# Three pairs of PSUM banks in the shared expert, and the last expert weights issued by SyncE

## The chip, the cores and the metric

The kernel runs on one core of a Trainium2 chip. A core has TensorE (matrix products into PSUM, eight banks), VectorE, ScalarE, GpSimd and SyncE, each with a queue of its own, and 16 DMA engines that all queues share. The metric is the device time of one execution in microseconds. The kernel before took 493.1 us (median of 3 runs, 491.43 to 493.35).

## The reference

Two cross-attention layers and two feed-forward layers over x of 2 x 1024 rows of 256 numbers. The change lies in the first feed-forward layer, a mixture of experts with a shared expert:

```python
gu = jnp.einsum('nh,eih->nei', x_flat, experts_gate_up)
g, u = (gu[..., :I], gu[..., I:])                      # I = 352, 8 experts, 2 chosen per row
h = jax.nn.silu(g) * u
expert_out = jnp.einsum('nei,ehi->neh', h, experts_down)
out = jnp.einsum('neh,ne->nh', expert_out, w)
shared = jax.nn.silu(x_flat @ shared_gate_w.T) * (x_flat @ shared_up_w.T) @ shared_down_w.T
out = out + sigmoid(x_flat @ shared_expert_gate_w.T) * shared   # 704 hidden columns
```

Everything is float32. The kernel writes each factor as the sum of a high and a low part in a faster format and adds three products.

## The kernel before

All queues are written out by hand. The 2048 rows are taken in four groups of 512. For the shared expert, a group has six steps (n counts them, 0 to 23): five of 128 hidden columns, with a gate and an up product of six matmuls each, and a half step (n = 5, 11, 17, 23) whose last 64 gate and 64 up columns share one product. `up(n)` issues them on TensorE (L1232, the half step L1226). Gate products go to bank n % 2 and up products to bank 2 + n % 2. In the first half (n below 12) ScalarE computes the silu (L1131) and copies the up product (L1137), and GpSimd multiplies. In the second half VectorE multiplies (L1475) the up product in its bank by the silu in SBUF. `down(g)` is the down product of a group (L1285), `add` the sum into x (L1426). down(0), steps 12 and 13, down(1), steps 14 to 23, down(2), down(3) follow each other on TensorE. Beside steps 12 to 23 GpSimd scatters the rows by expert into DRAM (`expert_rows_in`, 32 indirect DMAs, L1063).

The experts come next, in 39 blocks of 128 rows. For block b TensorE transposes the fetched rows (L960), ScalarE copies them as the high part (L966) and VectorE makes the low part (L971). `half` makes the gate, and later the up product: four matmuls with the high part (L1336, L1337) and two with the low part (L1340). ScalarE applies the silu (L1162), VectorE multiplies (L1496), TensorE transposes the result (L1348) and makes the down product (L1358 to L1362). TensorE's order in a turn is: gate of b, transposes of the hidden values of b - 1, transposes of the rows of b + 1, up product of b, down product of b - 1.

SyncE fetches the rows of a block (L953) and its weights and destinations (L954) into four buffers in turn: the fetch of block b waits for the transposes of block b - 4. The expert weights lie over buffers of the shared stage and so are loaded late. ScalarE's queue issues them (`load_w` L930, `load_d` L937): experts 0 to 3 after the last gate product, 4 after VectorE's last product, 5 after the scatters, and 6 and 7 after all down products (`d_ready` 16), behind the copy of block 0's rows and ahead of the first silu. GpSimd's queue loads the high parts of the down weights (L937). The low parts are made by a subtraction: of gate and up by L942, of down by L948, for expert 0 on VectorE, and else mostly on GpSimd.

Of the kernel before, what the change touches and what calls it, by code (L numbers as in the profile page):

```python
# [7 lines left out]
ALU = mybir.AluOpType  # L8
# [4 lines left out]
P = 128  # L13
# [15 lines left out]
KS = 6  # L29
# [25 lines left out]
def wait(engine, sem, value):  # L55

    if isinstance(value, int) and value <= 0:
        return
    if isinstance(sem, Event):
        engine.wait_ge(sem.sem, sem.before + value)  # L60
    else:
        engine.wait_ge(sem, value)
# [603 lines left out]
def xattn_ffn_kernel(nc, x_in, ctxT_in, wq0, wk0, wv0, wo0, gate_in, egu_in, edown_in, sgate_in, sup_in, sdown_in,  # L666
                     wq1, bq1, wk1, bk1, wv1, bv1, wo1, bo1, wr_in, a_in, bw_in, out):
    ctx = ExitStack()
    with ctx:
# [203 lines left out]
        NH = 2 * KS  # L873
        HIGH = slice(SR[5], P)

        def up_at(n):

            return (psum[n % 2], HIGH) if n % KS == KS - 1 else (psum[2 + n % 2], slice(0, P))

        def factor_rows(n):  # L880

# [2 lines left out]
        def ups(n):  # L884

            return n - n // KS
        act_s, up_s = mem["pw"][:, 0:2, :], mem["pw"][:, 2:4, :]
        hT = big[:, 0:2 * KS * SG].rearrange("p (b j n) -> p b j n", b=2, j=KS)

        xg = mem["xn"][:, :, :, :].rearrange("p b t n -> p (b t) n")  # L890
# [83 lines left out]
        def sync_on():  # L974
# [11 lines left out]
            sp.wait_ge(scattered, 16 * 2 * NT)  # L986
            for b in range(NX):
                fetch(sp, b)
            for b in range(NX, NB):
                fetch(sp, b)  # L990

# [131 lines left out]
        def scalar_on():  # L1123
            act = nc.scalar
            def silu(n):
                wait(act, g_ready, n + 1)
                if n < NH + 2:
                    wait(act, h_done, n - 1)
                else:
                    wait(act, h2_done, n - 1 - NH)  # L1130
                nc.scalar.activation(act_s[factor_rows(n), n % 2, :], psum[n % 2][0:SR[n % KS], :], ACT.Silu).then_inc(silu_done, 1)  # L1131

            def copy_up(n):

# [47 lines left out]
            load_w(act, 5, 6, w_in[4])  # L1182
            load_d(act, 5, 6, 1, w_in[4])
            copy_rows(0)
            act.wait_ge(d_ready, 16)
            load_w(act, 6, E, w_in[5])
            load_d(act, 6, E, 1, w_in[5])
            for b in range(NB):
                silu_rows(b)
                if b > 0:  # L1190
# [22 lines left out]
        def up(n):  # L1213

            g, j = n // KS, n % KS
            if g < 2:
                wait(nc.tensor, xL_ready, 2 * g + 2)
            wait(nc.tensor, silu_done, n - 1)
            if n < NH + 2:
                wait(nc.tensor, u_copied, n - 1)  # L1220
            else:
                wait(nc.tensor, h2_done, n - 1 - NH)
            terms = [(m, v, k) for k in range(KD) for m, v in ((sgu_hi, xn2T_hi), (sgu_hi, xn2T_lo), (sgu_lo, xn2T_hi))]
            if j == KS - 1:
                for a, (m, v, k) in enumerate(terms):
                    last = nc.tensor.matmul(psum[n % 2][:, :], m[:, k, 5 * P:6 * P], v[g][:, k, :],  # L1226
                                            start=(a == 0), stop=(a == len(terms) - 1))
                last.then_inc(g_ready, 1)
                return
            for w, bank, done in ((0, n % 2, g_ready), (1, 2 + n % 2, u_ready)):  # L1230
                for a, (m, v, k) in enumerate(terms):
                    last = nc.tensor.matmul(psum[bank][:, :], m[:, k, w * 6 * P + j * P:w * 6 * P + (j + 1) * P],  # L1232
                                            v[g][:, k, :], start=(a == 0), stop=(a == len(terms) - 1))
                last.then_inc(done, 1)

# [169 lines left out]
        def vector_on():  # L1405
# [64 lines left out]
            def hidden(n):  # L1470
                bank, rows = up_at(n)
                wait(dve, silu_done, n + 1)
                wait(dve, u_ready, ups(n + 1))
                wait(dve, d_ready, 4 * (n // KS - 1))
                v.tensor_tensor(hT[0:SR[n % KS], (n // KS + 1) % 2, n % KS, :], bank[rows, :],  # L1475
                                act_s[rows, n % 2, :], ALU.mult).then_inc(h2_done, 1)

            add(0)
            for n in range(2 * KS, 2 * KS + 2):
# [418 lines left out]
```

## Time and profile before

| | |
|---|---|
| median of 3 runs | 493.1 us (491.43 to 493.35) |
| profiled execution | 497.36 us, span 495.5 us |
| mean granted TensorE clock | 0.992 |
| TensorE busy (matmul) | 468.4 us, 95% of the span |
| VectorE, ScalarE, GpSimd busy | 58%, 40%, 48% |
| share of the DMA engines, 198 to 235 us | near full |

The profile comes from one execution. A timeline row gives the start, the length, the engine and line, the operation, and in brackets how long the engine stood idle before it and who released it. "remote" and "another core or an unknown queue" are releases that the profile can't assign. ACTq, POOLq and SPq are DMA issues of the queues of ScalarE, GpSimd and SyncE.

### The profile page before, as it was taken

The numbers are of one execution on the slowest core, as the hardware profiler recorded it, in microseconds if no ns is written. First come the engines' busy times: TensorE is split into PE (matmuls) and PEld (weight loads), VectorE is DVE, ScalarE is ACT, GpSimd is POOL, SyncE is SP. The second block draws the span as 40 slices with busy tenths as digits, with TensorE's granted clock in tenths as the row PEclk, the third lists the DMA queues.
The fourth block names the chain that finished last, engine by engine and source line by source line (L and its number), as shares of the span: only waits on it lengthen the run. The fifth ranks groups of instructions, "written<-read, shape, count | busy, mean of one in ns | idle before, by whom it ended". The sixth has DMA issues, their size and how long they took to land.

```text
span 495.5 us, 9491 instructions
## 1 busy us (share of the span) xinstructions
PE 468.4 (95%) x3132; PEld 385.0 (78%) x3132; DVE 286.6 (58%) x657; ACT 199.5 (40%) x447; POOL 236.0 (48%) x315
## 2 busy tenths in 40 slices
PE   7899999998999997998999999999997999899797
PEld 6677776686777786677999999999977676677576
DVE  5779985643461122325454545545457689998862
ACT  3455775557610021002323333232332456665641
POOL 6313344144337574219985543233232665753462
PEclk9999999999999999998999999999999899999999
DMA  8999300020003122999413332223117300000114
GB/s 280 392 404 351 41 12 1 1 85 2 0 1 111 69 103 84 340 309 331 70 48 102 108 87 70 82 65 86 34 42 238 104 2 1 1 3 0 31 34 150
DMA packets 48031, 52.98 MB, mean 107 GB/s; under 512 B 15313, under 2 KB 42258, under 8 KB 47730
## 3 DMA queue, kind: packets, MB, share of 16 engines
q1 hardware_dynamic: 34578, 23.02, 16.8%
q0 software_dynamic: 7616, 20.19, 12.3%
q10 hardware_dynamic: 5792, 9.18, 6.2%
q8 instruction: 28, 0.46, 0.4%
q14 instruction: 17, 0.14, 0.1%
HBM read 35.25 MB, written 17.12 MB: 106 GB/s over the span
## 4 chain that ended last, share of the span: by engine, by line
PE 75%; DVE 12%; ACT 4%; DMA 3%; issue 2%; another core or an unknown queue 1%; POOL 1%; ACTq 1%; SPq 0%; POOLq 0%; DVEq 0%
PE banks L1285 9%; PE banks L1232 9%; PE banks L1336 6%; PE banks L346 5%; PE banks L360 5%; PE banks L1337 5%; PE banks L1340 5%; PE banks L324 5%; PE banks L313 3%; PE banks L1358 3%; PE banks L1766 3%; PE banks L1362 3%; PE banks L1359 3%; PE banks L1348 3%; DVE mx L507 2%
## 5 line engine op out<-in xcount | busy, mean ns | idle before, releaser
L115 POOL TENSOR_TENSOR rstd<-var,mhalf 128x2 f32<-128x2 f32 x30 | 20.9, 696 | 86.1 <-DVE var L108 86.1
L1336 PE MATMUL banks<-w_hi,xgT_hi 128*128 x156 | 55.5, 356 | 2.8 <-ACT xgT_hi L966 2.3
L1162 ACT ACTIVATE hg<-banks 128x352 f32<-128x352 f32 x39 | 18.2, 466 | 98.6 <-PE banks L1340 89.0
L1509 DVE TENSOR_TENSOR hgT_lo<-banks,hgT_hi 128x256 fp32r<-128x256 f32 x78 | 24.1, 350 | 58.1 <-ACT hgT_hi L1169 56.7
L507 DVE TENSOR_REDUCE mx<-banks 128x16 f32<-128x1024 f32 x32 | 39.1, 1220 | 23.9 <-PE banks L324 23.7
L1337 PE MATMUL banks<-wd,xgT_hi 128*128 x156 | 51.0, 328 | 0.0
L1285 PE MATMUL banks<-sdn,big 128*128 128x256 f32 x192 | 47.5, 393 | 0.0
L1285 PEld LDWEIGHTS banks<-sdn,big 128*128 128x128 f32 x192 | 34.1, 189 | 12.6 <-issue 9.0
L1063 POOL DMA_INDIRECT expert_rows_in<-xn,slot x32 | 31.4, 982 | 20.7 <-issue 7.7
L324 PE MATMUL banks<-kvb,qT 64*128 64x256 f32 x256 | 36.7, 406 | 3.3 <-DVE ps L510 2.1
L1340 PE MATMUL banks<-w_hi,xgT_lo 128*128 x156 | 37.9, 325 | 0.0
L125 ACT ACTIVATE xn<-x,shift,rstd 128x256 f32<-128x256 f32 x60 | 32.9, 604 | 9.7 <-POOL shift L117 9.5
L1131 ACT ACTIVATE pw<-banks 128x512 f32<-128x512 f32 (+1 forms) x24 | 14.2, 593 | 53.0 <-issue 29.0
L1232 PE MATMUL banks<-xn2T_hi,sgu_hi 128*128 128x512 f32 x80 | 31.9, 399 | 2.9 <-DVE big L1475 2.9
L1336 PEld LDWEIGHTS banks<-w_hi,xgT_hi 128*128 128x128 f32 x156 | 29.9, 192 | 5.0 <-issue 4.5
L324 PEld LDWEIGHTS banks<-kvb,qT 64*128 64x128 f32 x256 | 22.5, 187 | 13.0 <-issue 9.1
L1094 POOL DMA_INDIRECT choices_out<-yy,dest x18 | 18.1, 1003 | 28.5 <-DVE yy L1502 21.1
L1232 PE MATMUL banks<-xn2T_lo,sgu_hi 128*128 128x512 f32 x80 | 31.2, 391 | 0.0
L1232 PE MATMUL banks<-xn2T_hi,sgu_lo 128*128 128x512 f32 x80 | 31.2, 390 | 0.0
L1358 PE MATMUL banks<-wd,hgT_hi 128*128 (+1 forms) x117 | 29.8, 284 | 0.7 <-ACT hgT_hi L1169 0.7
L1337 PEld LDWEIGHTS banks<-wd,xgT_hi 128*128 128x128 f32 x156 | 30.0, 192 | 0.2
L1359 PE MATMUL banks<-wd,hgT_hi 128*128 (+1 forms) x117 | 29.8, 283 | 0.0
(249 smaller groups left out, 1137.0 us busy)
## 6 DMA issues: line engine op xcount, KB each, us to landing
w_hi<-in_egu POOLq DMA_DIRECT2D x2, 2816.0 KB, 21.3
expert_rows_in<-zeros SPq DMA_DIRECT2D x1, 5304.0 KB, 40.3
xn<-expert_rows_in SPq DMA_DIRECT2D x39, 128.0 KB
y_all<-choices_out SPq DMA_DIRECT2D x16, 256.0 KB, 4.9
wd<-in_egu ACTq DMA_DIRECT2D x8, 352.0 KB, 9.7
wd<-in_egu ACTq DMA_DIRECT2D x4, 704.0 KB, 13.8
out_x<-x SPq DMA_DIRECT2D x8, 256.0 KB, 2.1
x<-in_x SPq DMA_DIRECT2D x2, 768.0 KB, 7.6
```

Of the source, the lines that this page charges most:

```text
L125: nc.scalar.activation(out[:, t, :], x[:, first + t, :], ACT.Identity, bias=m["shift"][:, b, t:t + 1], scale=m["rstd"][:, b, t:t + 1]).the ...
L324: last = nc.tensor.matmul(psS[:, r * 512 + hf * 256:r * 512 + hf * 256 + 256], qT[rows, u % 2, hf, t * P:(t + 1) * P], kb[batch_of(u)][row ...
L346: last = nc.tensor.matmul(psO[32 * j:32 * j + 32, k, w, :], lhs, pT[u % 2][:, 4 * k + j, :], start=True, stop=True, tile_position=(0, 32 * j))
L507: nc.vector.tensor_reduce(mx, heads(psS), AX.X, ALU.max).then_inc(max_done.sem, 1)
L1063: pool.indirect_dma_start(xg_dram[:, :], bass.IndirectOffsetOnAxis(ap=slot[:, j, t:t + 1], axis=0), xn2w[:, t, :], None, bounds_check=SLOT ...
L1232: last = nc.tensor.matmul(psum[bank][:, :], m[:, k, w * 6 * P + j * P:w * 6 * P + (j + 1) * P], v[g][:, k, :], start=(a == 0), stop=(a == ...
L1285: last = nc.tensor.matmul(psum[4 + c][:, t * D:(t + 1) * D], hT[0:SR[j], (g + 1) % 2, j, (2 * c + t) * P:(2 * c + t + 1) * P], sdn[0:SR[j] ...
L1336: nc.tensor.matmul(to, xgT_hi[:, c, k, :], hi, start=(k == 0), stop=False)
L1337: nc.tensor.matmul(to, xgT_hi[:, c, k, :], lo, start=False, stop=False)
L1340: last = nc.tensor.matmul(to, xgT_lo[:, c, k, :], w_hi[:, k, ds(e * (2 * I) + w * I, I)], start=False, stop=(k == KD - 1))
L1358: nc.tensor.matmul(psum[6][:, 0:D], h, d(k, 0), start=(k == 0), stop=False)
L1359: nc.tensor.matmul(psum[6][:, 0:D], h, d(k, 1), start=False, stop=False)
```

## The change

First, in steps 12 to 23 the gate and up products take three pairs of banks in turn (0 and 2, 1 and 3, 6 and 7) instead of two, and the silu takes three rows of its buffer. Banks 6 and 7 hold the router's ranks and logits before; step 14, the first to use them, waits for `routed`. The waits follow: a step waits for what step n - 3 left, not n - 2. Second, the gate, up and down weights of experts 6 and 7 (five DMAs) are issued by SyncE's queue, behind the fetches of blocks 0 to 3 and ahead of that of block 4. The wait for `d_ready` 16 goes with them.

```diff
+        def place(n):
+            return n % 2 if n < NH else n % 3
+        def gate_at(n):
+            return psum[(0, 1, 6)[place(n)]]
         def up_at(n):
-            return (psum[n % 2], HIGH) if n % KS == KS - 1 else (psum[2 + n % 2], slice(0, P))
+            return (gate_at(n), HIGH) if n % KS == KS - 1 else (psum[(2, 3, 7)[place(n)]], slice(0, P))
...
-        act_s, up_s = mem["pw"][:, 0:2, :], mem["pw"][:, 2:4, :]
+        act_s, up_s = mem["pw"][:, 0:3, :], mem["pw"][:, 2:4, :]
...
             for b in range(NX):
                 fetch(sp, b)
+            sp.wait_ge(d_ready, 16)
+            load_w(sp, 6, E, w_in[5])
+            load_d(sp, 6, E, 1, w_in[5])
             for b in range(NX, NB):
                 fetch(sp, b)
...
             def silu(n):
                 wait(act, g_ready, n + 1)
-                if n < NH + 2:
-                    wait(act, h_done, n - 1)
+                if n < NH + 3:
+                    wait(act, h_done, min(n - 1, NH))
                 else:
-                    wait(act, h2_done, n - 1 - NH)
+                    wait(act, h2_done, n - 2 - NH)
...
             copy_rows(0)
-            act.wait_ge(d_ready, 16)
-            load_w(act, 6, E, w_in[5])
-            load_d(act, 6, E, 1, w_in[5])
             for b in range(NB):
                 silu_rows(b)
...
-            wait(nc.tensor, silu_done, n - 1)
             if n < NH + 2:
+                wait(nc.tensor, silu_done, n - 1)
                 wait(nc.tensor, u_copied, n - 1)
+            elif n == NH + 2:
+                nc.tensor.wait_ge(routed, 1)
             else:
-                wait(nc.tensor, h2_done, n - 1 - NH)
+                wait(nc.tensor, silu_done, n - 2)
+                wait(nc.tensor, h2_done, n - 2 - NH)
```

The order of the products on TensorE is the same. On ScalarE's queue, from the weights of expert 5 to the first two blocks, there stood (`bt_ready` tells of transposed rows, `bg_ready` of a gate product):

```order
L930 DMA wd<-in_egu 128x704 [waits scattered]
L930 DMA wd<-in_egu 128x704
L937 DMA wd<-in_edown 128x256 x2
L937 DMA wd<-in_edown 96x256
L966 ACTIVATE xgT_hi<-banks 128x256 [waits bt_ready]
L930 DMA wd<-in_egu 128x2x704 [waits sh_d_ready]
L930 DMA wd<-in_egu 128x2x704
L937 DMA wd<-in_edown 128x2x256 x2
L937 DMA wd<-in_edown 96x2x256
L1162 ACTIVATE hg<-banks 128x352 [waits bg_ready]
L966 ACTIVATE xgT_hi<-banks 128x256 [waits bt_ready]
```

and now, with line numbers of the changed file, the same place on ScalarE:

```order
L939 DMA wd<-in_egu 128x704 [waits scattered]
L939 DMA wd<-in_egu 128x704
L946 DMA wd<-in_edown 128x256 x2
L946 DMA wd<-in_edown 96x256
L975 ACTIVATE xgT_hi<-banks 128x256 [waits bt_ready]
L1174 ACTIVATE hg<-banks 128x352 [waits bg_ready]
L975 ACTIVATE xgT_hi<-banks 128x256 [waits bt_ready]
```

The five issues and their wait are gone between the copy of block 0's rows and block 0's silu. On SyncE's queue, from block 3's fetch to block 5's, they now stand ahead of block 4's:

```order
L962 DMA xn<-expert_rows_in 128x256
L963 DMA slot_w<-expert_rows_in 128x2
L939 DMA wd<-in_egu 128x2x704 [waits sh_d_ready]
L939 DMA wd<-in_egu 128x2x704
L946 DMA wd<-in_edown 128x2x256 x2
L946 DMA wd<-in_edown 96x2x256
L962 DMA xn<-expert_rows_in 128x256 [waits bt_ready]
L963 DMA slot_w<-expert_rows_in 128x2
L962 DMA xn<-expert_rows_in 128x256 [waits bt_ready]
```

Before, the fetch of block 4 followed that of block 3 and waited only for the transposes of block 0.

## Rows read from the trace of the kernel before

**Rows 1.** Page, chain that ended last: shares of the span by engine.
```profile
PE 75%; DVE 12%; ACT 4%; DMA 3%; issue 2%; another core or an unknown queue 1%; POOL 1%; ACTq 1%; SPq 0%; POOLq 0%; DVEq 0%
```
**Rows 2.** Chain of waits in order of time: start, length, what.
```profile
182.28 6.31 another core or an unknown queue
```
**Rows 3.** Timeline of TensorE, 180 to 190 us: start, length, instruction, idle before.
```profile
180.96 0.39 PE L1232 MATMUL banks<-xn2T_hi,sgu_hi 128*128 128x512 f32 x1
...
183.68 0.39 PE L1232 MATMUL banks<-xn2T_hi,sgu_hi 128*128 128x512 f32 x1
...
186.18 0.39 PE L1232 MATMUL banks<-xn2T_hi,sgu_lo 128*128 128x512 f32 x1
189.51 0.47 PE L1232 MATMUL banks<-xn2T_hi,sgu_hi 128*128 128x512 f32 x1 [2.95 <-DVE big L1475]
```
**Rows 4.** Timeline of VectorE, 181 to 190 us.
```profile
188.67 1.34 DVE L1475 TENSOR_TENSOR big<-banks,pw 128x512 f32<-128x512 f32 x2 [6.39 <-remote]
```
**Rows 5.** Timeline of ScalarE, 183 to 190 us.
```profile
184.38 0.60 ACT L1131 ACTIVATE pw<-banks 128x512 f32<-128x512 f32 x1 [3.98 <-remote]
188.69 0.60 ACT L1131 ACTIVATE pw<-banks 128x512 f32<-128x512 f32 x1 [3.71 <-remote]
```
**Rows 6.** Timeline of TensorE, 222 to 236 us.
```profile
222.51 0.48 PE L1340 MATMUL banks<-w_hi,xgT_lo 128*128 x2
225.25 0.66 PE L1336 MATMUL banks<-w_hi,xgT_hi 128*128 x1 [2.26 <-ACT xgT_hi L966]
...
227.17 0.84 PE L1348 MATMUL banks<-ident,hh 128*128 128x128 f32 x3
...
235.70 0.38 PE L960 MATMUL banks<-ident,xn 128*128 128x128 f32 x2
```
**Rows 7.** Timeline of ScalarE and its DMA issues, 219 to 225 us.
```profile
219.09 0.39 ACT L966 ACTIVATE xgT_hi<-banks 128x256 fp32r<-128x256 f32 x1 [21.87 <-issue]
220.46 0.91 ACTq L930 DMA_DIRECT2D wd<-in_egu  x2
...
223.53 0.70 ACTq L937 DMA_DIRECT2D wd<-in_edown  x1
224.28 0.47 ACT L1162 ACTIVATE hg<-banks 128x352 f32<-128x352 f32 x1 [4.80 <-issue]
224.64 0.38 ACT L966 ACTIVATE xgT_hi<-banks 128x256 fp32r<-128x256 f32 x1
```
**Rows 8.** Timeline of VectorE, 202 to 226 us.
```profile
201.99 1.63 DVE L942 TENSOR_TENSOR wd<-wd,w_hi 128x1408 fp32r<-128x1408 f32 x1 [4.04 <-DMA wd<-in_egu]
...
221.54 3.95 DVE L948 TENSOR_TENSOR wd<-wd 128x512 fp32r<-128x512 f32 x2
225.42 0.41 DVE L971 TENSOR_TENSOR xgT_lo<-banks,xgT_hi 128x256 fp32r<-128x256 f32 x1
```
**Rows 9.** Timeline of GpSimd at 221 us.
```profile
221.45 3.17 POOL L942 TENSOR_TENSOR wd<-wd,w_hi 128x1408 fp32r<-128x1408 f32 x1 [20.27 <-DMA wd<-in_egu]
```
**Rows 10.** Windows: stretch, length, busy by engine, TensorE clock, DMA share, GB/s.
```profile
225.25:228.66 3.41, 3.41 (x13) 3.33 (x14) 1.04 (x4) 1.07 (x4) 3.00 (x4) 0.50 1.08 337
```
**Rows 11.** Timeline of SyncE's queue at 215 us.
```profile
214.69 0.32 SPq L953 DMA_DIRECT2D xn<-expert_rows_in  x1
```
**Rows 12.** DMA queues, 205 to 207 us; then an issue at 223.5: KB, us to landing.
```profile
q0 software_dynamic: 267, 0.27, 51.0%
q10 hardware_dynamic: 267, 0.27, 45.4%
q1 hardware_dynamic: 269, 0.12, 34.5%
...
wd<-in_edown ACTq DMA_DIRECT2D x1, 192.0 KB, 14.1
```
**Rows 13.** DMA queues, 219 to 222 us; then 224 to 232 us: packets, MB, share.
```profile
q1 hardware_dynamic: 287, 0.13, 15.9%
...
q10 hardware_dynamic: 1644, 2.58, 99.3%
```

More of the change, by code:

```diff
@@ L1126, in silu @@
                 wait(act, g_ready, n + 1)
-                if n < NH + 2:
-                    wait(act, h_done, n - 1)
-                else:
-                    wait(act, h2_done, n - 1 - NH)
-                nc.scalar.activation(act_s[factor_rows(n), n % 2, :], psum[n % 2][0:SR[n % KS], :], ACT.Silu).then_inc(silu_done, 1)
+                if n < NH + 3:
+                    wait(act, h_done, min(n - 1, NH))
+                else:
+                    wait(act, h2_done, n - 2 - NH)
+                nc.scalar.activation(act_s[factor_rows(n), place(n), :], gate_at(n)[0:SR[n % KS], :], ACT.Silu).then_inc(silu_done, 1)
             def copy_up(n):
@@ L1225, in up @@
                 for a, (m, v, k) in enumerate(terms):
-                    last = nc.tensor.matmul(psum[n % 2][:, :], m[:, k, 5 * P:6 * P], v[g][:, k, :],
+                    last = nc.tensor.matmul(gate_at(n)[:, :], m[:, k, 5 * P:6 * P], v[g][:, k, :],
                                             start=(a == 0), stop=(a == len(terms) - 1))
@@ L1229, in up @@
                 return
-            for w, bank, done in ((0, n % 2, g_ready), (1, 2 + n % 2, u_ready)):
+            for w, bank, done in ((0, gate_at(n), g_ready), (1, up_at(n)[0], u_ready)):
                 for a, (m, v, k) in enumerate(terms):
-                    last = nc.tensor.matmul(psum[bank][:, :], m[:, k, w * 6 * P + j * P:w * 6 * P + (j + 1) * P],
+                    last = nc.tensor.matmul(bank[:, :], m[:, k, w * 6 * P + j * P:w * 6 * P + (j + 1) * P],
                                             v[g][:, k, :], start=(a == 0), stop=(a == len(terms) - 1))
@@ L1475, in hidden @@
                 v.tensor_tensor(hT[0:SR[n % KS], (n // KS + 1) % 2, n % KS, :], bank[rows, :],
-                                act_s[rows, n % 2, :], ALU.mult).then_inc(h2_done, 1)
+                                act_s[rows, place(n), :], ALU.mult).then_inc(h2_done, 1)
             add(0)
```

## The prediction

> **What bounds the kernel now.** I read the chain of waits first, as shares and in order of time, then the timelines of TensorE, VectorE, ScalarE, GpSimd and SyncE from 178 to 240 us, then the DMA queues there. TensorE carries 75% of the chain [rows 1], so the question at each edit is whether TensorE stands idle and what would end its next idle time. Between 150 and 236 us it stands idle twice.
>
> The first gap is in the shared expert. The gate and up products of step n = 20 start at 183.68 and their last matmul at 186.18, and the first of n = 21 starts at 189.51, held 2.95 us by VectorE's product of n = 19 [rows 3]. Steps are numbered as in the code: 12 to 23 are the second half, 17 and 23 are half steps. The chain crosses this gap by a piece of 6.31 us that no engine owns [rows 2]. VectorE's step 19 began at 188.67, though ScalarE's silu of step 19 had ended at 184.98, and ScalarE's silu of step 20 began at 188.69 [rows 4, 5]. So both stood until 188.7 and then went on within 0.02 us of each other: a late signal held them. Whatever its origin, TensorE stopped because it was allowed only one step ahead of VectorE.
>
> The second gap is at the start of the experts. ScalarE copies block 0's rows at 219.09, then issues five weight DMAs from 220.46 to 224.24, and only then does block 0's silu (224.28) and block 1's copy (224.64) [rows 7]. TensorE is done with block 0's up product when its last two matmuls, started at 222.51, end near 222.99, and starts block 1 at 225.25, 2.26 us later [rows 6]. After that gap the granted clock is 0.50 (the 1.2 GHz level) for 3.41 us [rows 10]. Half of that, 1.7 us, is lost beside the gap.
>
> **Part 1, three pairs of banks.** Nothing is computed more or less. From n = 15 on TensorE waits for silu n - 3 and product n - 3 where it waited for n - 2. For n = 14 it waits for the slots, which the scatters that run here already use, so nothing. The third row of the silu buffer lies on a buffer that only the first half uses, and its wait (12 products of the first half) is met before the first down product. So the added waits cost 0 here, with a bound of one ScalarE silu, 0.60 us [rows 5], if one were late.
>
> What it removes: n = 21 would need VectorE's step 18, not 19. Step 18 ended before 182.3, since VectorE stood idle from then [rows 4]. So n = 21 starts with the end of n = 20. The pitch of a full step is 2.72 us (183.68 minus 180.96, [rows 3]), so n = 20 ends at 186.40 and n = 21 at 189.12. Late next is VectorE's step 19, needed by n = 22: 188.67 plus half of 1.34 us is 189.34, and the start followed the release by about 0.15 us (189.51 against 189.34), so n = 22 starts at 189.50. Before it started at 189.51 + 2.72 = 192.23. Gain 2.7 us. From below: if the late signal doesn't recur in an ordinary run, the other steps never waited for VectorE (one such wait in the whole half), and the gain is 0.
>
> ScalarE's weight loads start when n = 23 has its product, so they move with TensorE. The scatters on GpSimd are paced by its own queue and do not. GpSimd's loads of the down weights wait for them, so they gain less, and ScalarE's queue gets ahead of GpSimd's.
>
> **Part 2, the last weights from SyncE.** I use the clock of the trace before from here, and the 2.7 us stay beside it. ScalarE loses a wait and five issues, 3.78 us. Its silu of block 0 could then start with its gate, before the up product's last matmuls at 222.51 [rows 6], and block 1's copy 0.47 us later [rows 7], so TensorE's first four matmuls of block 1 need not wait. Late next is VectorE. It splits block 1's rows at 225.42, after the down weights of expert 0, which occupy it from 221.54 for 3.95 us [rows 8]; and the last two matmuls of block 1's gate need that split. So the gate's end moves from 227.17 to 225.42 + 0.41 + two matmuls (0.3 to 0.6 us, by clock), about 226.4 [rows 6, 8]. Gain 0.8 us, and the gap remains, only cut in two, so I give no clock back.
>
> From above: of the 3.95 us, GpSimd's weight split ran 221.45 to 224.62 [rows 9], while VectorE's own split of 1408 columns took 1.62 us [rows 8], so 512 columns should take about 0.6 us. They met by 0.09 us. If VectorE comes first, or GpSimd is done before, the whole gap goes: 2.3 us and the 1.7 us of the clock, 4.0 us. The Trainium skill (SBUF — State Buffer, section "SBUF: two separate sides") says that VectorE and GpSimd hold a shared port pair exclusively for a whole instruction; the trace agrees, with 3.95 us instead of about 1. By that rule the gain of this edit is 0.8 us or 4.0 us, depending on who starts first.
>
> What it adds: SyncE now waits for all down products (about 220.4) and issues five DMAs, 2.1 MB, before the fetch of block 4's rows, issued at 214.69 before [rows 11]. Queued behind them are the fetches of all later blocks. Block 4's transposes came at 235.70 [rows 6]; with 0.8 us gained they come at 234.9. When does its fetch land? A fetch issued at 214.69 moved its 287 packets between 219 and 222 [rows 11, 13], so about 4.3 us pass before a transfer starts here. A queue that is busy moved 2.58 MB in 8 us, 0.32 MB/us [rows 13], so 2.1 MB take 6.7 us. Lower bound: 220.46 + 4.3 + 6.7 = 231.5, hidden. But the same weights, issued by ScalarE, landed 14.1 us after the last issue, 223.53 + 14.1 = 237.6 [rows 7, 12], since three queues share the engines: in 205 to 207 us they moved 267, 267 and 269 packets, one each in turn [rows 12]. A fetch behind those weights can't be much before them, so 237.6 is the upper bound. SyncE's ring is empty and starts in parallel with the rest of ScalarE's, so I take a point two thirds up, nearer to the row of these very weights: 236.3, a stall of 1.4 us. Later fetches follow at once and are needed a whole block apart, so only block 4 waits.
>
> The Trainium skill (DMA: Bandwidth & Descriptors, section "Issuing engines are not separate DMA queues") says that DMAs issued by several engines interleave on the same 16 engines, and that issuing on more queues only saves the issuer's time. The equal packet counts agree. By it the weights land no earlier for being on SyncE, which speaks against this edit: it buys 3.78 us of ScalarE's time and sells the place of the row fetches.
>
> **The sum.** The profiled execution took 497.36 us (span 495.5, 1.9 around it). 497.36 - 2.7 (banks) - 0.8 (ScalarE freed) + 1.4 (block 4's fetch) = 495.3, 2.1 less. The median of the runs shown is 493.1, 4.3 below the profiled one. I carry the difference over: **491.0 us**, between 491.0 - 3.2 (VectorE comes first) and 491.0 + 2.7 (no late signal), widened by the fetch.
>
> **Rivals.**
> *The late signal belongs to the profiled execution.* For: it is 2.95 us, and ordinary runs are 4.3 us faster than the profiled one; VectorE is else held by nothing unnamed in this half. Against: nothing in the page marks it as foreign. Then part 1 gives 0, and 493.1 - 0.8 + 1.4 = 493.7; without the stall at block 4, 492.3.
>
> *The collision of VectorE and GpSimd goes away.* For: it hangs on 0.09 us, and ScalarE's queue runs ahead, so GpSimd's weights land and its split ends earlier. Against: then everything reaches block 4 earlier, and its fetch caps the gain; GpSimd also issues its second down weights earlier, into the same engines. 4.0 us less 2 of a longer stall instead of the net -0.6: 493.1 - 2.7 - 2.0 = 488.4.
>
> *The row fetch costs more than all else gives (slower).* SyncE's queue puts block 4's rows at 237.6 or later, TensorE waits 2.7 us or more at its transposes, and the idle time is followed by the lower clock as at 225.25, another 1.7 us. 493.1 - 0.8 + 2.7 + 1.7 = 496.7 without the late signal, 494.0 with it. It decides when the fetch lands after 235.7 plus what part 1 gave. For: the lower clock did follow a 2.26 us gap. Against: after the 2.95 us gap the clock stayed at 1.00, in the shared stage's denser work, and SyncE's ring is empty at its start.
>
> **How the numbers follow.** Forecast (489.5 to 492.3): 0.43. Late signal absent (491.8 to 494): 0.28. Collision gone: 0.14. Fetch outweighs: 0.15. The predicted time is the first's. The range 488.0 to 494.6 takes in the second and third and most of the fourth; the likeliest's own range is 489.5 to 492.3. A measurement tells 0.5% (2.5 us) from no change, so faster means under 490.6. The forecast has 0.18 of its 0.43 there, the collision case all 0.14: with 0.02 of the rest, 0.34. Slower means over 495.6: 0.13 from the fetch case, and 0.03 from the second. The remaining 0.50 is the same.
>
> **What would show it.** Part 1: no idle of TensorE over 1 us in the second half, although VectorE or ScalarE may still show an unnamed wait; if none shows and none is idle either, the late signal was not of the kernel. Part 2: ScalarE's silu of block 0 within 0.5 us of its gate; VectorE's first down split of about 4 us (collision) or 1 us (none); a wait of TensorE at the transposes of block 4 for a DMA, 1 to 2 us. The prediction is wrong if block 4's rows are there in time and the time is above 492.5, or if TensorE waits for rows of block 5 or later.

## The result, and the profile after

The changed kernel took 497.88 us (median of 20 runs), the kernel before 493.17 us (20 runs of the same session): a ratio of 1.009, 95% interval 1.0067 to 1.0113. It is slower, 3.3 us above the upper end of my range. The ratio leaves out two slower runs of the changed kernel, one of 773.93 us at a mean clock of 0.556 and the profiled one. The profiled execution of the changed kernel took 501.21 us (span 499.4), 3.3 above its median, so its losses are larger than the usual ones; the experiments below show the same pattern in other executions.

First its chain of waits, as shares of the span, which answers to [rows 1]:
```profile
PE 69%; DVE 11%; DMA 9%; ACT 4%; issue 3%; POOL 2%; SPq 0%; POOLq 0%; ACTq 0%; DVEq 0%
```
DMA went from 3% to 9% of the chain. The timeline of TensorE at the start of the experts, which answers to [rows 6], with its only idle time of the stretch from 140 to 242 us:
```profile
221.22 0.32 PE L1349 MATMUL banks<-wd,xgT_hi 128*128 x1
229.69 0.95 PE L1352 MATMUL banks<-w_hi,xgT_lo 128*128 x2 [8.14 <-DVE xgT_lo L980]
```
The chain in order of time (start, length, what) says what stood behind VectorE's low copy:
```profile
195.54 5.66 DMA expert_rows_in<-xn,slot
201.20 0.29 issue
201.49 1.84 POOL wd L946 x2
203.33 24.82 DMA wd<-in_edown
...
228.27 0.13 DVE wd L957
```
Read it backwards. Block 1's gate wants VectorE's split of its rows; VectorE stands at the down split of expert 0, in order ahead of it, until all of GpSimd's first load of high down weights (experts 0 to 4, three transfers, 1.76 MB in all, under one semaphore) has landed; GpSimd issued it only when the last scatter of rows had landed, 5.66 us after its issue. VectorE, GpSimd, and ScalarE's queue in their timelines:
```profile
228.27 1.02 DVE L957 TENSOR_TENSOR wd<-wd 128x512 fp32r<-128x512 f32 x2 [8.88 <-DMA wd<-in_edown]
229.22 0.41 DVE L980 TENSOR_TENSOR xgT_lo<-banks,xgT_hi 128x256 fp32r<-128x256 f32 x1
```
```profile
195.54 0.97 POOL L1075 DMA_INDIRECT expert_rows_in<-xn,slot  x1 [0.30 <-issue]
201.49 2.63 POOL L946 DMA_DIRECT2D wd<-in_edown  x3 [4.98 <-DMA expert_rows_in<-xn,slot]
```
```profile
194.69 1.86 ACTq L939 DMA_DIRECT2D wd<-in_egu  x4
```
Before, the last scatter was issued at 194.49, ahead of ScalarE's first load at 196.64, and GpSimd issued the down weights at 198.55. Now ScalarE's load starts at 194.69 and the last scatter at 195.54. The order of the two has turned. The last of the three transfers took 24.8 us from issue to landing, where it took 19.4 before:
```profile
wd<-in_edown POOLq DMA_DIRECT2D x1, 480.0 KB, 24.8
```
And the clock behind the gap, as in [rows 10]; the eighth column is the granted clock, so TensorE ran at 1.2 GHz until 235.7:
```profile
230.00:232.00 2.00, 2.00 (x9) 1.92 (x9) 0.17 (x2) 1.15 (x4) 2.00 (x3) 0.50 0.22 52
232.00:234.00 2.00, 2.00 (x9) 2.00 (x9) 1.27 (x4) 0.13 (x1) 1.99 (x4) 0.50 0.68 145
234.00:236.00 2.00, 2.00 (x11) 2.00 (x11) 0.58 (x2) 0.00 (x0) 2.00 (x3) 0.57 1.25 298
```
The account between the two profiled executions, from TensorE's starts: up to the first down product +1.3 us; from there to the end of the up products 57.8 to 54.6, -3.2; from there to block 4's transposes 39.3 to 46.0, +6.7; behind them 259.8 to 258.9, -0.9. Together +3.9, the 3.85 between 501.21 and 497.36. So one stretch was 3.2 us shorter, and the next lost twice as much. The 3.2 us are not yet a gain of the banks: in this execution no engine saw the late signal of [rows 2, 3, 4, 5]. VectorE's products of the second half start with the ordinary wait throughout:
```profile
187.94 0.69 DVE L1487 TENSOR_TENSOR big<-banks,pw 128x512 f32<-128x512 f32 x1 [2.03 <-PE banks L1244]
190.66 0.69 DVE L1487 TENSOR_TENSOR big<-banks,pw 128x512 f32<-128x512 f32 x1 [2.03 <-PE banks L1244]
```
Two pairs of banks without that signal are as fast there, as the experiments show.

### The profile page after: what moved, and what is told of

It reads as the page before. It is cut to its first block, busy times and chain, and to the rows that moved or that the text cites. A ratio compares the mean times of both kernels' runs of the same rounds, so it can differ in the third digit from the quotient of the medians.

```text
span 499.4 us, 9490 instructions
## 1 busy us (share of the span) xinstructions
PE 470.3 (94%) x3132; PEld 386.8 (77%) x3132; DVE 284.0 (57%) x657; ACT 199.4 (40%) x447; POOL 236.0 (47%) x315
## 4 chain that ended last, share of the span: by engine, by line
PE 69%; DVE 11%; DMA 9%; ACT 4%; issue 3%; POOL 2%; SPq 0%; POOLq 0%; ACTq 0%; DVEq 0%
PE banks L1244 8%; PE banks L1348 5%; PE banks L346 5%; PE banks L1352 5%; PE banks L360 5%; DMA wd<-in_edown 5%; PE banks L324 5%; PE banks L1349 5%; PE banks L1297 5%; PE banks L313 3%; PE banks L1370 3%; PE banks L1374 3%; PE banks L1371 3%; PE banks L1778 3%; PE banks L1360 3%
## 5 line engine op out<-in xcount | busy, mean ns | idle before, releaser
L1521 DVE TENSOR_TENSOR hgT_lo<-banks,hgT_hi 128x256 fp32r<-128x256 f32 x78 | 24.1, 351 | 56.8 <-ACT hgT_hi L1181 56.8
L1352 PEld LDWEIGHTS banks<-w_hi,xgT_lo 128*128 128x128 f32 x156 | 27.5, 191 | 8.4 <-DVE xgT_lo L980 8.4
```

Of the source, the lines that this page charges most:

```text
L1352: last = nc.tensor.matmul(to, xgT_lo[:, c, k, :], w_hi[:, k, ds(e * (2 * I) + w * I, I)], start=False, stop=(k == KD - 1))
```

## Experiments

All ratios are against the kernel before on the same chip, with the 95% interval. "Expected" is what stood on record before the run.

**Each part alone.** First part 1 alone: the weights' three lines go back to ScalarE.
```
-            sp.wait_ge(d_ready, 16)
-            load_w(sp, 6, E, w_in[5])
-            load_d(sp, 6, E, 1, w_in[5])
...
+            act.wait_ge(d_ready, 16)
+            load_w(act, 6, E, w_in[5])
+            load_d(act, 6, E, 1, w_in[5])
```


> The changed kernel with its second part undone: the last weights are issued by ScalarE again. Theory (the high down weights of expert 0 land late for two reasons: ScalarE's weight loads start before the last scatter is down and stretch it, so GpSimd's loads start late; and SyncE's queue takes a third of the packets from them): the first reason stays, the second goes. The last scatter takes about 5.7 us to land as in the changed kernel (2.5 us before), the down weights land 22 us after their issue instead of 24.8, TensorE waits 3 to 6 us instead of 8.1 in block 1, and the time is 494 to 497 us. Rival A (SyncE's share alone is the cause): no wait over 2.5 us, 490 to 492.5 us. Rival B (the bank change alone is the cause): 497 to 499 us.

Measured: 1.0059 [1.003, 1.0088]. ScalarE's first load at 195.32, last scatter at 196.39, down weights issued at 202.54 and 23.6 us to landing; TensorE idle 2.9 and 4.1 us in block 1. It also stood idle for 1.83 us in the shared stage, at a late signal that three pairs did not pass. So most of the loss comes with the banks.

Then part 2 alone: the kernel before, with the three lines on SyncE.

> The kernel before with only the second part: the last weights issued by SyncE, two pairs of banks. Theory: the scatter is down in about 2.5 us when no late signal delays or frees TensorE, GpSimd's down weights start in time but share the engines with SyncE's weights; they land 0 to 3 us later than before (220.1), TensorE waits 0 to 3 us: 492 to 495 us. Rival A (SyncE's share alone is the cause): as slow as the changed kernel, 497 to 499 us. Rival B (the bank change alone): 492 to 493.5 us.

Measured: 1.0005 [0.9983, 1.0028], no difference. The scatter (195.53) was ahead of the load (197.52), and the same 480 KB landed 19.6 us after their issue, at 220.8. SyncE issued its weights only at 221.31, so this run does not test what a third queue does to that landing; it shows that part 2 alone leaves the order as it was and costs nothing.

**Changing the order.** Two edits of the changed kernel: ScalarE's first load waits for all scatters; and SyncE's weights wait for GpSimd's down weights.
```
             act.wait_ge(g_ready, 4 * KS)
+            act.wait_ge(scattered, 16 * 2 * NT)
             load_w(act, 0, 1, w_in[0])
```


> The changed kernel, with ScalarE's first weight load waiting until all scatters have landed, as GpSimd's loads do. Theory: the last scatter lands in about 2.5 us instead of 5.7, GpSimd's down weights are issued about 3 us earlier, and since ScalarE's queue no longer has a head start they land at the same distance or less: TensorE's wait shrinks from 8.1 to 2 to 5 us, 493 to 496 us. Rival A (SyncE's share alone): the wait stays over 6 us, 497 to 499 us. Rival (the loads are simply too many for the time): every load starts later, nothing gained, 498 us or more.

```
             sp.wait_ge(d_ready, 16)
+            sp.wait_ge(d_hi_in[0], 16 * KI)
             load_w(sp, 6, E, w_in[5])
```


> The changed kernel, with SyncE holding the last weights back until GpSimd's first high down weights have landed. Theory: they land 2 to 3 us sooner than in the changed kernel; TensorE waits 5 to 6 us instead of 8.1, but the fetch of block 4's rows behind SyncE's weights is now late by several us, so the time is 496 to 500 us with a new wait at the transposes of block 4. Rival A (SyncE's share alone): the wait of block 1 falls under 2.5 us. Rival C (neither; the weights are late by their late issue alone): the landing stays at about 228.

Measured: 1.0081 [1.0048, 1.0114] and 1.0043 [1.0012, 1.0073]. In the first, the down weights landed in 17.6 us, but the load began at 201.21, 6.5 us later, and TensorE waited 3.4 us at the end of the shared stage and 2.1 in block 1: the time moved to another transfer. The last scatter did not land in the 2.5 us that I expected but in 4.5, with no load beside it. From 197 to 199 us there stood beside the scatter's own packets one packet of queue 8, of which the part on why the scatters came late tells more:
```profile
q0 software_dynamic: 88, 0.25, 33.9%
q8 instruction: 1, 0.02, 3.9%
```
In the second, SyncE issued its weights at 229.07, just behind the landing of the down weights, whose last transfer took 21.2 us instead of 24.8. TensorE still waited 4.4 us for the low copy, and 1.9 us for the rows of block 0; the wait at block 4 that I expected did not come. Neither removed the loss. A gentler version, where ScalarE's first load waits for the last VectorE product of the shared stage (1.5 us later), did restore the scatter's landing:
```
+            act.wait_ge(h2_done, 2 * KS)
```


> The changed kernel, with ScalarE's first weight load waiting for VectorE's last product, some 1.5 us later than now. Theory (these loads, begun before the last scatter is down, stretch it from 2.5 to 5.7 us and so hold back GpSimd's down weights): the last scatter lands 1 to 2 us earlier against its issue, the down weights 1 to 2 us earlier, TensorE waits 6 to 7 us instead of 8.1, and the time is 0.1 to 0.4% under the changed kernel. Rival (the start of ScalarE's loads doesn't matter to the scatter): the same landing and time as the changed kernel.

Measured: 1.0081 [1.0056, 1.0106]. The last scatter (195.77) came ahead of the load (196.62), and 2.46 us behind it SyncE fetched. But ScalarE, behind its later issues, copied block 0's rows only at 219.95, and TensorE had four waits of 0.6 to 2.3 us. With the order mended by holding ScalarE back, the time was no better than the changed kernel's. That the four waits are what took the gain is argued from this one profile.

**The wait itself.** VectorE needs expert 0's 352 KB alone. GpSimd's first load is split, and VectorE waits for the first piece, in the changed kernel, in part 1 alone, and in the kernel before.
```
-            load_d(pool, 0, 5, 0, d_hi_in[0])
+            load_d(pool, 0, 1, 0, d_hi_one)
+            load_d(pool, 1, 5, 0, d_hi_in[0])
...
-            dve.wait_ge(d_hi_in[0], 16 * KI)
+            dve.wait_ge(d_hi_one, 16 * KI)
```


> The changed kernel, with the high down weights of expert 0 as a transfer of their own (352 KB) ahead of those of experts 1 to 4, and VectorE waiting for that transfer alone. Theory (TensorE's 8.1 us wait in block 1 is VectorE waiting for the last of 1.76 MB, of which it needs 0.35): they land 5 to 8 us after their issue, before VectorE is ready for them near 219.4; the wait of block 1 falls under 1 us and the time to 489 to 492 us on a chip where the kernel before takes 493, 0.3 to 0.9% under it. If block 4's rows are late then, it is a wait of 1 to 4 us at its transposes, and the time is within 0.3% of the kernel before. Rival (VectorE's wait is not on the critical path; the time goes elsewhere): as slow as the changed kernel.

> Three pairs of banks alone (last weights on ScalarE) with the same split of the first down weights. Theory: the wait for VectorE's down split goes, what stays is the wait of 2.3 to 2.9 us for ScalarE's copy of block 1's rows, behind its five issues, and the lower clock behind it: 0.0 to 0.5% under the kernel before, 0.6 to 1.0% under the bank change alone. Rival (the bank change costs by something other than the down weights): as slow as the bank change alone, 0.6% over the kernel before.

> The kernel before with the same split and nothing else. There the down weights landed at 220.1 and VectorE wanted them at 221.5, so theory says nothing is gained: within 0.3% of the kernel before. If the landing varies from run to run around that time, 0.2 to 0.5% are gained, and part of what the changed kernel lost was lost in some runs of the kernel before too.

Measured: 1.0013 [0.9988, 1.0038], 1.0003 [0.9982, 1.0024] and 1.0009 [0.9985, 1.0032]. The split takes the loss of 0.9 and 0.6% away and is worth nothing to the kernel before, whose profile has no wait for the landing. The second has the turned order in its profile (ScalarE's load at 193.19, last scatter at 193.37, landed 5.1 us later), and still TensorE waits only for ScalarE's copy, which stands behind its five issues as before:
```profile
221.84 0.42 PE L1349 MATMUL banks<-w_hi,xgT_hi 128*128 x1 [2.46 <-ACT xgT_hi L975]
```
The profile of the first does not show the late landing: there the scatter (192.68) was ahead of the load (193.82). Its wait in block 1 is 2.25 us and not under 1, as I had expected, for VectorE's down split met GpSimd's again. Block 4's rows are now late, as I had forecast; its TensorE timeline:
```profile
223.66 0.89 PE L1353 MATMUL banks<-w_hi,xgT_lo 128*128 x2 [2.25 <-DVE xgT_lo L980]
...
235.41 0.44 PE L969 MATMUL banks<-ident,xn 128*128 128x128 f32 x2 [1.89 <-DMA slot_w<-expert_rows_in]
```
The third holds a second finding: with two pairs of banks and no late signal, the stretch from the first down product to the last up product took 54.56 us; with three pairs it took 54.55. Two pairs lose time there only where a signal comes late.

**The scatter alone.** The kernel before, with its last two scatters held until the last gate product, so that they are issued with ScalarE's first load and nothing else changes.
```
                     pool.wait_ge(*product_of(j * NT + t))
+                    if j == 1 and t == NT - 2:
+                        pool.wait_ge(g_ready, 4 * KS)
```


> The kernel before, with one wait more on GpSimd: the last two scatters of rows are issued after the last gate product of the first half, so about when ScalarE's first transfer of expert weights is under way. Nothing else is changed: two pairs of banks, the last weights on ScalarE. Theory (a last scatter that is issued behind the start of the weight transfers lands 4 to 6 us after its issue in place of 2.5, and all of GpSimd's down weights stand behind it): the down weights are issued 3 us or more later than before, TensorE waits 3 to 8 us in block 1, and the time is 0.5 to 1.0% above the kernel before. Rival (only the third queue's share of the packets makes the down weights late): no wait over 2.5 us in block 1 and within 0.3% of the kernel before.

Measured: 1.0153 [1.0111, 1.0195]. GpSimd, VectorE and TensorE in its timelines:
```profile
195.37 0.98 POOL L1065 DMA_INDIRECT expert_rows_in<-xn,slot  x1 [0.30 <-issue]
202.44 2.62 POOL L937 DMA_DIRECT2D wd<-in_edown  x3 [6.09 <-DMA expert_rows_in<-xn,slot]
```
```profile
227.36 1.02 DVE L948 TENSOR_TENSOR wd<-wd 128x512 fp32r<-128x512 f32 x2 [8.96 <-DMA wd<-in_edown]
```
```profile
222.00 0.42 PE L1338 MATMUL banks<-w_hi,xgT_hi 128*128 x1 [2.11 <-ACT xgT_hi L966]
228.77 0.95 PE L1342 MATMUL banks<-w_hi,xgT_lo 128*128 x2 [5.86 <-DVE xgT_lo L971]
```
With two pairs of banks and without the third queue, the late scatter alone makes the whole pattern, and a larger loss than the change. So a late scatter, issued behind the start of the load, is enough for 8 us of idle TensorE; 2.1 of them, ScalarE's copy, the kernel before has too. The rival, that the third queue's share is needed for it, fell. The loss is above the 0.5 to 1.0% that I expected, and part of it is the edit's own: it issues the last scatter 56.8 us after the first down product, where it was 53.5 in the two profiles of two pairs without a late signal. That lateness alone is not what stretches the landing: in part 2 alone the last scatter was issued at 195.53, no earlier than here, but ahead of the load, and landed in 2.46 us.

**The changed kernel again.**

> The changed kernel again, unchanged, beside the three others on one chip. Theory: 0.6 to 1.2% above the kernel before, the last scatter lands 5 us or more after its issue, and TensorE waits about 8 us in block 1 for the low copy of the rows behind VectorE's down split. Rival (the 8 us belong to one profiled execution, and the time is lost in many small places): the wait of block 1 is under 3 us while the time is still 0.6 to 1.2% above.

Measured: 1.0082 [1.005, 1.0113], but the profiled execution, at 493.55 us, was the fastest of its eight (the others 496.6 to 499.4). It shows what a good execution has in another way:
```profile
192.56 0.97 POOL L1075 DMA_INDIRECT expert_rows_in<-xn,slot  x1 [0.30 <-issue]
195.74 2.62 POOL L946 DMA_DIRECT2D wd<-in_edown  x3 [2.21 <-DVE big L1487]
```
```profile
193.83 1.80 ACTq L939 DMA_DIRECT2D wd<-in_egu  x4
```
```profile
222.36 0.59 PE L1352 MATMUL banks<-w_hi,xgT_lo 128*128 x2 [1.68 <-DVE xgT_lo L980]
232.71 0.44 PE L969 MATMUL banks<-ident,xn 128*128 128x128 f32 x2 [2.01 <-DMA slot_w<-expert_rows_in]
```
The scatter was 1.3 us ahead of the load, the down weights landed in 19.3 us (at 216.9, before SyncE issued its weights at 217.64), and the granted clock was 1.00 from 230 to 234. In wording the rival of this run came half true (a wait under 3 us), but at a time 7.7 us under the 501.21: in the two profiled executions of one and the same kernel the wait and the time go together.

The executions side by side (us; the fourth number is from the last scatter's issue to SyncE's first fetch, which waits for its landing):
```
                     last     ScalarE's   scatter  down w.  TensorE idle
                     scatter  first load  landed   issued   in block 1    ratio
before               194.49   196.64      2.46     198.55   2.3           1
part 2 alone         195.53   197.52      2.46     199.44   2.0           1.0005
changed, again       192.56   193.83      2.46     195.74   1.7           (493.55 us)
changed              195.54   194.69      5.68     201.49   8.1           1.009
part 1 alone         196.39   195.32      5.87     202.54   2.9 + 4.1     1.0059
scatter held         195.37   193.29      6.79     202.44   2.1 + 5.9     1.0153
```
Over all 17 profiles, in the nine where ScalarE's load began first the scatter landed in 5.1 to 7.1 us; in the eight where the scatter was first it took 2.5, but for the 4.5 above. GpSimd's down weights pay a second time for ScalarE's head start. Where they are one load, their last transfer landed in 17.6 us when it was issued 0.2 us behind ScalarE's first load, in 19.3 to 20.5 us at 1.9 us behind it (four profiles), and in 21.1 to 26.1 us at 6.4 to 9.2 us behind it (six profiles). How much of this last range is the share of SyncE's queue is open: with two queues at work it was 23.0 and 23.6, with SyncE held back 21.2, and the time with SyncE held back, 1.0043, is under the 1.0082 and 1.009 of the changed kernel, with overlapping intervals.

**Why the scatters came late.** GpSimd waits for its first sixteen scatters before the next sixteen. In the five profiles with two pairs this wait was 2.5 us; in seven of the nine so far with three pairs it was 4.0 to 4.6. GpSimd at this place in the changed kernel, and the packets of the queues from 170 to 175 us:
```profile
170.73 0.97 POOL L1075 DMA_INDIRECT expert_rows_in<-xn,slot  x1 [0.73 <-PE banks L1297]
175.33 0.21 POOL L1070 COPY xn<-tag 128x32 f32<-128x32 f32 x1 [3.62 <-DMA expert_rows_in<-xn,slot]
```
```profile
q0 software_dynamic: 96, 0.28, 15.5%
q8 instruction: 1, 0.02, 1.1%
```
Queue 8 moves 28 packets and 0.46 MB in all, 16 KB each, about one for each 256 instructions of TensorE: its own program. With three pairs its ninth packet fell 1.6 to 2.4 us after the sixteenth scatter's issue, each time beside the scatter's own packets; with two pairs 3.9 to 11.3 us after. Why it falls earlier with three pairs I did not find out. The next run moves it by added waits that are long met, ahead of 48 products; a second puts as many in blocks 14 to 25.
```
                 for a, (m, v, k) in enumerate(terms):
+                    if 1 <= n < 5:
+                        nc.tensor.wait_ge(sgu_split, 8)
+                        nc.tensor.wait_ge(shared_in, 80)
```


> The changed kernel with two waits more, on semaphores that are long complete, ahead of each of 48 products of shared units 1 to 4: 48 to 96 instructions more in TensorE's program before the second half. Theory (a packet of TensorE's own instructions beside the sixteenth scatter stretches its landing, and all scatters behind it come 2 us late): the packet that stood at 171 to 173 us comes 6 to 12 us earlier, GpSimd's wait between the sixteenth and seventeenth scatter is 2.5 us in place of 4.6, the last scatter is issued 53.5 us after the shared stage's first down product in place of 55.6 and lands in 2.5 us, the wait of block 1 falls from 8 us to under 3, and the time is within 0.3% of the kernel before. Rival (the waiting has another reason, of the banks' own): the gap of 4.0 us or more stays, and the time stays 0.6 to 1.2% above the kernel before.

```
+                    if 14 <= b < 26:
+                        nc.tensor.wait_ge(sgu_split, 8)
+                        nc.tensor.wait_ge(shared_in, 80)
```


> The changed kernel with the same two waits ahead of 48 products of expert blocks 14 to 25: as many instructions more, but behind the shared stage, so that the packet at 171 to 173 us stays where it is. Theory: like the changed kernel, 0.6 to 1.2% above the kernel before (added instructions cost nothing beside the products), GpSimd's wait before the seventeenth scatter 4.0 us or more in the likelier case. Rival (any added instructions change the time): a time that differs from the changed kernel's by more than 0.3%.

Measured: packet moved 1.0007 [0.9969, 1.0044] (by the medians, 498.44 and 496.42, 1.004); packet kept 1.0138 [1.0081, 1.0196]. GpSimd in the first, then in the second:
```profile
171.89 0.21 POOL L1070 COPY xn<-tag 128x32 f32<-128x32 f32 x1 [1.52 <-DMA expert_rows_in<-xn,slot]
...
189.35 0.97 POOL L1075 DMA_INDIRECT expert_rows_in<-xn,slot  x1 [2.70 <-PE banks L1247]
...
194.45 0.97 POOL L1075 DMA_INDIRECT expert_rows_in<-xn,slot  x1 [0.30 <-issue]
200.25 2.62 POOL L946 DMA_DIRECT2D wd<-in_edown  x3 [4.82 <-DMA expert_rows_in<-xn,slot]
```
```profile
174.13 0.21 POOL L1070 COPY xn<-tag 128x32 f32<-128x32 f32 x1 [3.36 <-DMA expert_rows_in<-xn,slot]
```
The packet came at 164.2 and the idle time of GpSimd there fell from 3.62 to 1.52 us, as it does again in the last run below (1.51), so the packet did stretch the scatter. But my expectation of this run held only in part. The last scatter was still late in the profiled execution, since another wait of 2.70 us, for a product of TensorE, came ahead of the scatter at 189.35; the wait of block 1 was 4.0 us, not under 3. The kernel before has the same wait, 2.63 us, at the same scatter. VectorE and TensorE in this run:
```profile
188.66 1.94 DVE L1490 TENSOR_TENSOR big<-banks,pw 128x512 f32<-128x512 f32 x3 [6.42 <-remote]
```
```profile
189.49 0.47 PE L1247 MATMUL banks<-xn2T_hi,sgu_hi 128*128 128x512 f32 x1 [0.26 <-DVE big L1490]
```
In the kernel before, the late signal held the shared stage up as well, so ScalarE's loads moved with the scatters. With three pairs the shared stage passes the late signal, the loads start on time and the scatters do not. That is a second way to the same turn of the order, and it comes out of the very gain that I had forecast. The kept packet's profile shows the long wait (3.36), a late signal that stopped TensorE for 2.27 us in the shared stage, and 9.8 us of idle TensorE in block 1; it is slower than I expected from the changed kernel, and how much of that surplus is the late signal's is not known. Which of the two ways the unprofiled executions took is open too.

**All mended.** The changed kernel with the split, block 4's fetch ahead of SyncE's weights, and GpSimd's first split of down weights behind VectorE's; and the same with two pairs of banks; and the first again with the added waits in the shared stage.
```
+            fetch(sp, NX)
             sp.wait_ge(d_ready, 16)
...
-            for b in range(NX, NB):
+            for b in range(NX + 1, NB):
...
             pool.wait_ge(lo_made, 2)
+            pool.wait_ge(d_lo_made, 1)
```


> The changed kernel with three edits: GpSimd's first transfer of high down weights brings expert 0's alone and signals by itself, and VectorE waits for that one; SyncE issues the fetch of block 4 ahead of the last expert weights; GpSimd starts its first split of down weights after VectorE's low copy of expert 0 is made. Theory (the changed kernel lost its time because VectorE waited for 1.76 MB though expert 0's 352 KB is all that block 1 wants, and in a smaller part because block 4 is fetched behind the weights): no wait of TensorE over 2.5 us between the shared stage's end and block 4, the down split about 1.0 us long, and a time 0.5 to 1.2% under the kernel before. Rival (the third queue's packets slow whatever stands beside them, so something else is late): the waits come back elsewhere in blocks 1 to 4, and the time is within 0.4% of the kernel before.

> The same three edits, with the last expert weights on SyncE, but with two pairs of PSUM banks for gate and up as in the kernel before. Theory (three pairs save time only in an execution with a late signal): equal to the one with three pairs within 0.3%, the stretch from the first down product to the last up product 54.5 us, or 57 to 58 us where a signal comes late. Rival (three pairs are worth the 2.7 us of my forecast): 0.4 to 0.7% slower than the one with three pairs.

> The kernel with the split transfer of down weights, the earlier fetch of block 4 and GpSimd's later split, with the 48 places of added waits in shared units 1 to 4 as well. Theory (once VectorE waits for expert 0's down weights alone, a late scatter is hidden): within 0.3% of the same kernel without the added waits, which was 0.8% under the kernel before. Rival (the scatter's landing still costs, at block 0's rows): 0.3 to 0.6% faster than without them.

Measured: 0.992 [0.9888, 0.9952], 0.9975 [0.9949, 1.0] and 0.9882 [0.9835, 0.9928]. The first is faster than both kernels (median 490.15 us against 493.93 for the kernel before). Its scatter was late too, and no longer costs; VectorE's split, and TensorE's one idle time from 140 to 262 us:
```profile
218.07 1.02 DVE L957 TENSOR_TENSOR wd<-wd 128x512 fp32r<-128x512 f32 x2
```
```profile
231.48 0.38 PE L1373 MATMUL banks<-wd,hgT_hi 128*128 x1 [2.12 <-POOL wd L957]
```
The third is 0.4% below the first by its ratio, with overlapping intervals, on another chip: too close to tell my expectation (within 0.3%) from its rival (0.3 to 0.6% faster). The second was expected equal to the first and is 0.5% slower (492.46 us, 2.3 more), as the rival said, although the two profiled executions agree (spans 489.0 and 488.6, the shared stretch 54.56 and 54.55). Neither profile has the late signal, so it would be a matter of the other executions; I did not profile one of them, and that the 2.3 us are its price is argued, not shown.

## Why the prediction was wrong

**The step that failed** is the third paragraph of part 1: "GpSimd's loads of the down weights wait for them, so they gain less, and ScalarE's queue gets ahead of GpSimd's." I saw the order turn and gave it no price: the sum has no term for it. The trace of before had the two facts that it needed. The down weights landed at 219.8, and VectorE was free for them at 221.5, a slack of 1.7 us; and VectorE's down split stands in order ahead of block 1's low copy. I took VectorE's start at 221.54 [rows 8] as fixed by its own work. In place of that zero the profile of the changed kernel has the down weights issued 2.9 us later and their last transfer 5.4 us longer on its way. They landed at 228.15, TensorE stood idle for 8.1 us, and 6.0 us of work at half the clock followed. Net of what the stretch lost before that is 6.7 us. The time lost in part 1 alone is 0.6%, in the change 0.9%, and the split transfer takes both away.

The reason that I gave for the turn was right for some executions only. In the changed kernel's profile ScalarE's load did not gain on TensorE's products: it began 54.8 us after the first down product, as with two pairs and no late signal. The scatters were 2.1 us late, behind the stretched sixteenth. In the run with the packet moved it was as I had written, with one difference: the scatters are not paced by GpSimd's queue alone. Each waits for a product of TensorE, and the late signal held them.

**Part 1, the banks, -2.7.** By the sign that I had set, the changed kernel's profile belongs to the first rival: no idle time of TensorE and no unnamed wait, so no late signal. Its 3.2 us in the shared stretch are the absence of the signal, for two pairs need 54.56 us without it and three 54.55. My bound of zero was needed. Where the signal comes, the mechanism is right. In the run with the packet moved VectorE stood for 6.42 us, against 6.39 before [rows 4], and TensorE for 0.26 instead of 2.95, starting again at 189.49, where I had forecast 189.50 for step 22. The last product of the stage ended at 193.84 instead of 196.60, with the first down product at 138.6 in both. The forecast of 2.7 us is met there. It is not a rule: in part 1 alone and with the packet kept, VectorE went on only at 192.83 and 193.79, and TensorE stood for 1.83 and 2.27 us with three pairs too.

**Part 2, ScalarE freed, -0.8.** The mechanism was right: ScalarE's silu of block 0 came at 219.67, and block 1's copy 0.36 us behind it. It gained nothing because VectorE was late by far more. The down split took 1.02 us and not 3.95: GpSimd's split had run at 214.74, so the collision was gone, as the second rival had it, and hid behind the landing. In the good execution of the changed kernel it was there again in part, 3.41 us, and TensorE's wait in block 1 was 1.68 us instead of 2.26.

**Block 4's fetch, +1.4.** Hidden in the profiled execution, since block 4 came at 240.49 instead of 234.9. This, with a time above 492.5, is one of the two signs by which I had called the prediction wrong. Where the wait for the down weights is away it is 1.89 and 2.01 us, 0.5 and 0.6 more than my point and within my bounds (0 to 2.7); in part 2 alone, behind another wait of 1.96 us, it is 0.35.

**The slower rival** named the right outcome for the wrong transfer. 496.7 was its time; that the measured one is only 1.2 higher is luck. My range ended at 494.6, and so it took in little of that rival (494.0 to 496.7), not most of it, as I wrote.

**The sum.** 497.36 - 3.2 + 6.7 + the 1.3 and -0.9 of the rest is the profiled execution's 501.2, to a rounding. That is an account of where the two profiles differ and no test of a forecast. My carrying over of the 4.3 us between profile and median came out near, by this one case: the changed kernel's profile lies 3.3 above its median.

## What to carry to other kernels

When an edit brings one queue's start forward, look for every transfer that used to be issued ahead of it, and work out the slack of what waits for that transfer; a slack of under 2 us, as here, leaves little room for a move. A consumer should wait for the bytes that it uses: one semaphore over 1.76 MB, where 352 KB were wanted, cost the changed kernel 0.8% (1.009 against 1.0013 with the transfer split). And profile a second execution of a kernel whose runs spread by more than 1%; the order of two issues can differ between them.

## What the runs showed of the hardware

- An indirect scatter of rows (2.46 us from issue to the next queue's release) took 5.1 to 7.1 us when ScalarE's weight transfers had begun before it, in nine profiles. From 197 to 199 us in the changed kernel, ScalarE's queue moved 265 packets beside the scatter's 48:
```profile
q10 hardware_dynamic: 265, 0.66, 85.4%
q0 software_dynamic: 48, 0.14, 17.2%
```
 The Trainium skill (DMA: Bandwidth & Descriptors, section "Issuing engines are not separate DMA queues") has all queues interleave on the same engines, and these rows agree; that a small transfer pays for it with more than twice its landing time is what the runs add.
- A 16 KB packet of TensorE's instructions beside a scatter stretched that scatter's landing: its last packet started 3.1 to 4.0 us after the issue instead of 2.06, in eight of the ten executions where they met. TensorE had no idle time beside it. The Trainium skill (Runtime: NRT & Kernel Launch, section "Instruction fetch mechanics") gives blocks of 16 KiB or 256 instructions and calls the cost of crossing one mostly hidden; the size agrees with the 28 packets here, and for TensorE so does the rest, but not for the transfer beside it.
- After 8.14 us without work the granted clock was 0.50 for 6.0 us of full work (229.7 to 235.7), longer than the 3.41 us after the gap of 2.26 us [rows 10].
